# Attention by pairs of heads: the weighted products one half later in TensorE's order, three buffers for the split probabilities

## What is computed

```python
q = query @ w_q
kv = context @ w_kv
k, v = jnp.split(kv, 2, axis=-1)
q = q.reshape(B, NQ, NUM_HEADS, HEAD_DIM).transpose(0, 2, 1, 3)
k = k.reshape(B, NKV, NUM_HEADS, HEAD_DIM).transpose(0, 2, 1, 3)
v = v.reshape(B, NKV, NUM_HEADS, HEAD_DIM).transpose(0, 2, 1, 3)
scores = jnp.einsum('bhqd,bhkd->bhqk', q, k) * SCALE
attn = jax.nn.softmax(scores, axis=-1)
out = jnp.einsum('bhqk,bhkd->bhqd', attn, v)
out = out.transpose(0, 2, 1, 3).reshape(B, NQ, INNER)
return out @ w_out + b_out
```

## Time and profile before

| | us |
|---|---|
| median of 3 runs | 2040.35 (2038.81 to 2043.65) |
| the profiled execution | 2027.9, its span 2026.1 |
| TensorE busy in the span | 1749.6 (86%) |
| VectorE, ScalarE, GpSimd busy | 1321.2, 1276.9, 1167.1 |
| of GpSimd's, low probabilities of this attention (L1089) | 290.8 in 256 instructions |
| granted clock of TensorE, mean | 0.918 |

### The profile page before, as it was taken

One profiled execution on the slowest core, in us unless ns is written; L12 is line 12 of the kernel. 1 busy time (PEld: TensorE's weight loads), 2 busy tenths in 40 slices (PEclk: granted clock), 3 DMA queues, 4 the chain that ended last, 5 costly groups with the idle time before them and its releaser, 6 DMA issues. The chain is left out here.

```text
span 2026.1 us, 55231 instructions
## 1 busy us (share of the span) xinstructions
PE 1749.6 (86%) x22101; PEld 1217.8 (60%) x22101; DVE 1321.2 (65%) x2620; ACT 1276.9 (63%) x1664; POOL 1167.1 (58%) x1089
## 2 busy tenths in 40 slices
PE   7997479999377599999999999999766738999778
PEld 3444258888366256666666666666536627888645
DVE  7774879998543675556565555565364547888765
ACT  5765358888343267777777777777644527888553
POOL 8411046666423367777777777777661337886434
PEclk9988689999588599999999999999878869999899
DMA  5232000000410200000000000000122111000000
GB/s 150 59 72 35 0 2 3 3 3 3 137 51 15 59 12 11 11 11 13 13 11 12 11 11 12 14 11 8 49 79 54 37 49 38 3 3 3 2 6 17
DMA packets 97217, 55.20 MB, mean 27 GB/s; under 512 B 43469, under 2 KB 90904, under 8 KB 96966
## 3 DMA queue, kind: packets, MB, share of 16 engines
q1 hardware_dynamic: 92662, 44.40, 8.6%
q0 software_dynamic: 3584, 6.36, 1.0%
q10 hardware_dynamic: 720, 0.92, 0.2%
HBM read 30.16 MB, written 13.75 MB: 22 GB/s over the span
## 5 line engine op out<-in xcount | busy, mean ns | idle before, releaser
L1663 POOL TENSOR_TENSOR aw_p_lo<-aw_p,aw_p_hi 128x512 f16<-128x512 f32 x512 | 575.9, 1155 | 189.3 <-issue 170.2
L1679 DVE TENSOR_REDUCE aw_max_part<-ps 128x1 f32<-128x512 f32 x512 | 351.2, 690 | 283.0 <-PE ps L1483 277.8
L1614 ACT ACTIVATE aw_p<-ps 128x1024 f32<-128x1024 f32 x256 | 260.0, 1016 | 199.1 <-PE ps L1514 196.9
L1089 POOL TENSOR_TENSOR ap_p_lo<-ap_p,ap_p_hi 128x512 f16<-128x512 f32 x256 | 290.8, 1156 | 148.0 <-issue 142.4
L1528 PE MATMUL ps<-ctx_hi_lo,aw_p_hi 128*128 128x97 f16 x2048 | 288.7, 206 | 2.5 <-POOL aw_p_lo L1663 2.5
L1530 PE MATMUL ps<-ctx_hi_lo,aw_p_hi 128*128 128x96 f16 x2048 | 287.8, 207 | 0.0
L1532 PE MATMUL ps<-ctx_hi_lo,aw_p_lo 128*128 128x97 f16 x2048 | 287.2, 204 | 0.0
L1621 ACT ACTIVATE aw_p_hi<-aw_p 128x1024 f16<-128x1024 f32 x256 | 270.6, 1057 | 8.1
L1530 PEld LDWEIGHTS ps<-ctx_hi_lo,aw_p_hi 128*128 128x128 f16 x2048 | 197.7, 97 | 25.2
L1528 PEld LDWEIGHTS ps<-ctx_hi_lo,aw_p_hi 128*128 128x128 f16 x2048 | 196.3, 96 | 12.2 <-POOL aw_p_lo L1663 4.7
L1483 PE MATMUL ps<-ctxT_hi,aw_queries 96*128 96x512 f16 x512 | 197.2, 390 | 5.2 <-DVE aw_max_part L1679 4.4
(11 more groups left out here) (524 smaller groups left out, 4939.4 us busy)
## 6 DMA issues: line engine op xcount, KB each, us to landing
sf_weights_raw<-in_L_w SPq DMA_DIRECT2D x24, 256.0 KB, 4.1
slot_scratch<-x_normT SPq DMA_DIRECT2D x16, 260.0 KB, 3.9
sf_fetched<-slot_scratch SPq DMA_DIRECT2D x16, 260.0 KB, 2.9
sf_weights_raw<-in_L_w SPq DMA_DIRECT2D x8, 512.0 KB, 3.8
x_norm<-result_scratch SPq DMA_DIRECT2D x8, 256.0 KB, 3.9
aw_queries<-aw_queries SPq DMA_DIRECT2D x32, 64.0 KB, 1.9
aw_queries<-aw_q_lo SPq DMA_DIRECT2D x32, 64.0 KB, 2.0
aw_queries<-aw_queries SPq DMA_DIRECT2D x32, 36.0 KB
```

Of the source, the lines that this page charges most:

```text
L1089: nc.gpsimd.tensor_tensor(p_lo[:, i % 2, h, :], p[:, i % 2, h, :], p_hi[:, i % 2, h, :], ALU.subtract).then_inc(lo_done, 1)
L1614: nc.scalar.activation(p[:, n % 2, :].rearrange("p (b q) -> p b q", b=2), s, ACT.Exp, scale=1.0 / QS).then_inc(exp_done, 1)
L1663: nc.gpsimd.tensor_tensor(p_lo[:, n % 4, cols], p[:, n % 2, cols], p_hi[:, n % 4, cols], ALU.subtract).then_inc(lo_done, 1)
L1679: nc.vector.tensor_reduce(mpart[:, b % 2, k:k + 1], ps[:, max_bank(b, k), :], AX.X, ALU.max).then_inc(m_done, 1)
```

## The change

TensorE's step i now does weighted(i-1) in place of weighted(i), and what follows from a half's weighted product moves along: VectorE does normalised(i-2) in place of normalised(i-1); turn, turned, project and the addition to x come one unit (two steps) later. `max_rows(i+2)` still stands between the two heads of the weighted product of the same step. `p_hi` and `p_lo` get three buffers (`PR`), so `highs` and GpSimd wait for the weighted product three halves back; in steps that product is as far back as before. The steps end two later. `p` keeps two buffers. No instruction is added or removed. All lines of the changed kernel from L1013 on are numbered one higher.

```diff
+    PR = 3
-        p_hi, p_lo = sb("p_hi", [P, 2, 2, QB], F16), sb("p_lo", [P, 2, 2, QB], F16)
+        p_hi, p_lo = sb("p_hi", [P, PR, 2, QB], F16), sb("p_lo", [P, PR, 2, QB], F16)
-        steps = range(-3, NH + 3)
+        steps = range(-3, NH + 5)
 # GpSimd
-                    if i >= 2:
-                        pool.wait_ge(av_done, i - 1)
+                    if i >= PR:
+                        pool.wait_ge(av_done, i - PR + 1)
...
 # TensorE
                 def values(u):
-                    if u >= 2:
-                        pe.wait_ge(t_done, u - 1)
+                    if u >= 3:
+                        pe.wait_ge(t_done, u - 2)
...
-                        if h == 1 and is_half(i + 2):
-                            max_rows(i + 2)
+                        if h == 1 and is_half(i + 3):
+                            max_rows(i + 3)
...
                 def turn(u):
-                    pe.wait_ge(v_done, min(u + 2, NU))
+                    pe.wait_ge(v_done, min(u + 3, NU))
...
-                    if i % 2 == 0 and is_unit(i // 2 - 1):
-                        turn(i // 2 - 1)
+                    if i % 2 == 0 and is_unit(i // 2 - 2):
+                        turn(i // 2 - 2)
-                    if is_half(i + 2) and not is_half(i):
+                    if is_half(i + 2) and not is_half(i - 1):
                         max_rows(i + 2)
-                    if is_unit((i - 3) // 2):
-                        project((i - 3) // 2, 1 - i % 2)
-                    if is_half(i):
-                        weighted(i)
+                    if is_unit((i - 5) // 2):
+                        project((i - 5) // 2, 1 - i % 2)
+                    if is_half(i - 1):
+                        weighted(i - 1)
 # ScalarE, highs; its turned moves as turn does
-                    if i >= 2:
-                        act.wait_ge(av_done, i - 1)
+                    if i >= PR:
+                        act.wait_ge(av_done, i - PR + 1)
 # VectorE; its turned and add move by two steps as well
-                    if is_half(i - 1):
-                        normalised(i - 1)
+                    if is_half(i - 2):
+                        normalised(i - 2)
```

More of the change, by code:

```diff
@@ L1085, in _ @@
                     pool.wait_ge(hi_done, i + 1)
-                    if i >= 2:
-                        pool.wait_ge(av_done, i - 1)
+                    if i >= PR:
+                        pool.wait_ge(av_done, i - PR + 1)
                     for h in range(2):
-                        nc.gpsimd.tensor_tensor(p_lo[:, i % 2, h, :], p[:, i % 2, h, :], p_hi[:, i % 2, h, :],
+                        nc.gpsimd.tensor_tensor(p_lo[:, i % PR, h, :], p[:, i % 2, h, :], p_hi[:, i % PR, h, :],
                                                 ALU.subtract).then_inc(lo_done, 1)
@@ L1181, in weighted @@
                                 v, vl = V_hi[:, u % 2, 2 * j + kt, h, 0:65], V_lo[:, u % 2, 2 * j + kt, h, :]
-                                nc.tensor.matmul(o, p_hi[:, i % 2, h, cols], v, start=h + t + kt == 0, stop=False,
+                                nc.tensor.matmul(o, p_hi[:, i % PR, h, cols], v, start=h + t + kt == 0, stop=False,
                                                  skip_group_check=True)
-                                nc.tensor.matmul(o[:, 0:64], p_hi[:, i % 2, h, cols], vl, start=False, stop=False,
+                                nc.tensor.matmul(o[:, 0:64], p_hi[:, i % PR, h, cols], vl, start=False, stop=False,
                                                  skip_group_check=True)
-                                ins = nc.tensor.matmul(o, p_lo[:, i % 2, h, cols], v, start=False, stop=kt == 1,
+                                ins = nc.tensor.matmul(o, p_lo[:, i % PR, h, cols], v, start=False, stop=kt == 1,
                                                        skip_group_check=True)
@@ L1244, in highs @@
                     act.wait_ge(exp_done, i + 1)
-                    if i >= 2:
-                        act.wait_ge(av_done, i - 1)
-                    nc.scalar.activation(p_hi[:, i % 2], p[:, i % 2], ACT.Copy).then_inc(hi_done, 1)
+                    if i >= PR:
+                        act.wait_ge(av_done, i - PR + 1)
+                    nc.scalar.activation(p_hi[:, i % PR], p[:, i % 2], ACT.Copy).then_inc(hi_done, 1)
                 def queries_keys(i):
@@ L1275, in _ @@
                         queries_keys(i + 3)
-                    if i % 2 == 0 and is_unit(i // 2 - 1):
-                        turned(i // 2 - 1)
+                    if i % 2 == 0 and is_unit(i // 2 - 2):
+                        turned(i // 2 - 2)
                     if i % 2 and is_unit((i + 1) // 2):
@@ L1349, in _ @@
                         max_rows(i + 2)
-                    if i % 2 == 0 and is_unit(i // 2 - 1):
-                        turned(i // 2 - 1)
+                    if i % 2 == 0 and is_unit(i // 2 - 2):
+                        turned(i // 2 - 2)
                     if i % 2 and is_unit((i + 1) // 2):
                         values((i + 1) // 2)
-                    if i % 2 == 0 and is_unit(i // 2 - 2) and (i // 2 - 2) % NP == NP - 1:
-                        add((i // 2 - 2) // NP)
+                    if i % 2 == 0 and is_unit(i // 2 - 3) and (i // 2 - 3) % NP == NP - 1:
+                        add((i // 2 - 3) // NP)
         retire(nc, sems)
```

## The result

The changed kernel takes 2025.83 us (median of 5 runs, 2020.83 to 2029.05), the kernel before 2040.35 (median of 5, 2035.21 to 2043.65). The ratio is 0.9936 with a 95% interval of 0.9912 to 0.9961: 14.5 us or 0.64% less, where 12.5 us were predicted and the range was 2022 to 2035.5.

The account below looks back on a forecast made before the run. TensorE's own work was taken to bound the second layer's steady part, a two-step ring through GpSimd's low parts the fourth's kept pairs. 2.8 + 4.5 + 5.2 = 12.5 us off 2040.35 gave 2027.8, range 2022 to 2035.5.

Parts of the forecast that it names:

- The ceiling of 18.5 us: Whole span: all TensorE waits for the low probabilities, weight loads 9.7 us and matmuls 8.8 us, 0.9% of the time.
- Steady parts: Second layer 0; fourth layer's kept pairs from 6.89 to 6.62 us, 5.2 us gained after 0.2 off for GpSimd's weight split.
- A: Fourth layer's weight split: GpSimd's idle 0.24 us cannot be used, nine pairs stay at 6.88, 2030.0 us; chance 0.12.
- Start of the second layer: Second layer's first steps: waits of 1.15 and 0.6 us go, 1.1 moves to the end, 0.1 off; 2.8 us gained.
- Start of the fourth layer: Fourth layer's first steps: waits of 2.20, 0.46 and 0.9 us go, 1.1 moves; 4.7, kept as 4.5 for GpSimd's lateness.
- Ends: Last exponential to last turn: moved work is covered while low parts are awaited, chain keeps its length, 0 us.
- C: Ends of both calls: TensorE's clock holds at 2.4 GHz, 1.1 us a call, 2.2 in all, 2025.6 us; chance 0.17.
- The sum: Both calls: 2.8 + 4.5 + 5.2 = 12.5 us gained, as it stands; chance 0.50.
- The offset of 12.45 us: Whole kernel: median of runs is 12.45 us longer than the profiled execution, taken to hold for the changed kernel too.
- B: Steady part: the ring closes in another place with a wait of the same size, only starts gain 7.3, 2033.0; chance 0.10.
- D: All 128 halves: VectorE's maxima, with 0.13 us of margin, come late; 19.5 us slower, 2059.9 us; chance 0.04.
- E: Whole kernel: nothing to be measured, pauses not the low parts' or both ends lengthen by 1.9 us, 2037 to 2040; chance 0.07.

Follow-up runs that it names:

- the delayed pair of kernels: One more GpSimd subtraction of 256 columns ahead of each half's low parts, in the kernel before (ratio 1.0219) and in the changed kernel (0.9977), both against the kernel before.

## Why the prediction was right, and where it wasn't

The time and the direction were right. Step by step:

- *The ceiling of 18.5 us was a wrong sum.* It adds the waits of the weight loads and those of the matmuls, and ten of them are one idle time listed twice. The matmul at 282.75 waited 0.45 us, and its weight load stood idle through the same time:

```profile
282.74 0.10 PEld L1182 LDWEIGHTS ps<-ap_v_hi,ap_p_hi 128*128 128x128 f16 x1 [0.60 <-POOL ap_p_lo L1089]
```

  Counted once, the 31 and 14 waits are 14.8 us. Of these 4.1 lie behind the last exponentials of the two calls, where the moved work now fills them without making the chain shorter. 10.7 us could be gained from waits, and the 2.2 us of moved work were never among them. The low end of the range, 2021.9, was built on the 18.5. The forecast itself was not: its terms go place by place. In the changed kernel no wait of TensorE for the low parts is left; part of the time at the starts goes to waiting for VectorE.
- *Steady parts: right.* Predicted 0 in the second layer, 6.62 us a pair with kept keys; measured 0.06 over 19 pairs, and 6.61 (6.74 in two of 19). The 0.2 us taken off because GpSimd needs 6.64 under the weight split didn't appear: the pairs there take 6.61 too, so GpSimd's own need is at most that and had been estimated at least 0.03 too high, and its idle 0.24 could be used. A is refuted by the same row.
- *Start of the second layer: the mechanism was right, its size depends on the clock.* Predicted 2.8, measured 1.6 in the first comparison, 2.6 where the clock rises at the same moment. The prediction took the clock's moment as given; one profile can't show that it varies.
- *Start of the fourth layer: mis-sized.* Predicted 4.5 us, measured 22.23 - 19.09 = 3.1. From exponential 1 to 3 it gains 8.12 - 5.67 = 2.45, nearly the 2.66 of the removed waits. From 3 to 6 it gains 10.65 - 9.53 = 1.12, where 0.9 + 1.1 were expected. From 0 to 1 it loses 3.89 - 3.46 = 0.43, since the clock rose later by about 1 us; before, the wait for the low parts behind it took such a delay up (the kernel with the third buffer alone has 3.89 too, and 22.25 from 0 to 6). The term that was sized wrong is VectorE's row of operations: "about 2.8 in all, an estimate". The changed kernel's VectorE timeline shows a start step in which it never idles:

```profile
1698.29 1.23 DVE L1302 TENSOR_REDUCE ap_neg_max<-ps 128x4 f16<-128x1024 f32 x1 [0.57 <-PE ps L1129]
...
1701.41 1.23 DVE L1302 TENSOR_REDUCE ap_neg_max<-ps 128x4 f16<-128x1024 f32 x1
```

  1701.41 - 1698.29 = 3.12 us, which is what the exponentials 4 to 6 stand apart (3.12 and 3.11), not TensorE's own 2.84. In the step before it TensorE waits for the maxima:

```profile
1696.45 0.23 PE L1166 MATMUL ps<-ident,ap_neg_max 128*128 128x128 f16 x1 [0.57 <-DVE ap_neg_max L1302]
```

  The wait for `p`, which the prediction did foresee, is there as well, 0.82 us at 1692.16.
- *The last exponential: not counted.* The last exponential follows its predecessor after 3.11 us in both calls; in the kernel before it was 3.51 and 3.52. No queries and keys are made in these last steps, so TensorE has less to do and had waited there for the low parts as in the kept part:

```profile
504.26 0.10 PEld L1182 LDWEIGHTS ps<-ap_v_hi,ap_p_hi 128*128 128x128 f16 x1 [0.36 <-POOL ap_p_lo L1089]
```

  This row of the kernel before was there to be read, and is worth 0.41 us a call.
- *Ends: predicted 0, measured 1.05 and 1.27.* The chain kept its length (6.17 and 6.20 us), so the cover held. The gain is the clock's: C was true, and its price of 1.1 a call was right. The prediction gave it 0.17 and left it out of the sum.
- *The sum.* By calls 2.8 + 9.7 + 0 was predicted. Measured 2.0 + 8.9 from the first to the last exponential, 2.3 at the ends, and 0.2 lost ahead of the first exponential of the second layer, 13.0. **The sum came out close because two errors have opposite signs**: the starts gave 2.6 us less than predicted (1.4 of it by the moment of the clock), ends and last steps gave 3.1 more. That the number came so close is luck to that extent.
- *The offset of 12.45 us.* It was assumed that the changed kernel's profiled execution would lie as far under its median as the profile of before did. It lay 1.7 us above its own (2027.53 against 2025.83). The difference of medians didn't need the assumption, only the number given for the profiled execution did.
- *B, D and E.* B is refuted by the delayed pair of kernels, E by the waits and by the fourth call's 10 us. D occurs only in the two pairs with an addition into `x` (0.26 us in all). In the other turning steps VectorE's maxima end at 1722.39, for example, and TensorE asks for them at 1722.52, the same 0.13 us as before.

## What to carry to other kernels

A pause that returns every other step, while the engine that it hits is nearly full and the others have room, can be a ring, as it was here: ask how many steps lie between producing a tile and the place where the bounding engine wants it, and put the consumer one step later in that engine's order. A further buffer does nothing while the order still asks for the tile at once (0 us here), and the order does nearly everything with the old buffers (12.1 of 13.0 us). Before betting on such a change look at the engine that is next in line, here VectorE with 6.23 us of work in 6.61, and at each place where the bounding engine idles at the end of a stage: what fills it may hold its clock, worth about 1.1 us there.

## What the runs showed of the hardware that was not expected

**A VectorE copy from SBUF to SBUF waits for GpSimd.** Alone two copies of 128 x 128 in f32 took 0.35 us; beside GpSimd's two subtractions a pair took 1.90 us and ended 0.09 us after them. The median of a single copy was 611 ns against 209 at the least. VectorE's maxima, which read PSUM, are not held up: in the changed kernel the one at 1717.74 took 1.23 us wholly beside the GpSimd row at 1717.20 (2.27), and all 128 lie between 1214 and 1227 ns. GpSimd's own low parts stayed at 2.27 for two. The Trainium skill (SBUF — State Buffer, SBUF: two separate sides) says that VectorE and GpSimd share one pair of SBUF ports, which is locked for a whole instruction, that an f32 copy within SBUF is one of VectorE's operations that take it, and that the other engine is blocked meanwhile. These rows agree, with GpSimd as the one who came first. For this kernel it means that VectorE's work may not be moved from PSUM to SBUF lightly: one such pair a half made the two calls 92 us longer than the changed kernel's.

**The moment at which the clock rises differs where the code is the same.** In the second layer's call it rose either before the first exponential or about 2 us after it, and the same six steps took 1.0 us more in the second case (21.7 and 22.7 in the order of before, 19.1 and 20.1 in the new one). Two profiles of two kernels can differ by that alone. What sets the moment is left open, and so is whether it varies between executions of one kernel: the only kernel profiled twice fell into the late case twice. In the two kernels that filled TensorE's idle time ahead of this call the granted clock was 1.00 through the whole start, and the six steps took 19.04 and 19.19 us.

**A wait of 25.8 us can cost nothing.** It is ScalarE's, in the kernel with two buffers, on an engine that would have idled one instruction later anyway: its pairs take 6.61 us as without the wait.
